# A fused cross-attention, mixer and mixture-of-experts block: weighing ahead of the scores in a head slot, and the split of keys and values moved

## The reference

```
Q = (layernorm(x) @ Wq.T + bq);  K = ctx @ Wk.T + bk;  V = ctx @ Wv.T + bv
weights = softmax(Q K^T / sqrt(32))          # per batch and head, 128 x 2048
x = x + (weights V) @ Wo.T + bo
```

## Time and profile before

| | |
|---|---|
| median of 3 executions | 2321.56 us (2314.86 to 2323.9) |
| the profiled execution, its own time | 2320.49 us |
| its span in the trace | 2318.7 us |
| attention slots of batches 0 to 6 | about 151 to 1091 us of the span |
| attention slots of the last batch | about 1091 to 1241 us |
| PE busy over the span | 1967.2 us (85%) |
| VectorE, GpSimd, ScalarE busy | 1543.6, 1149.4, 804.4 us |

### The profile page before, as it was taken

How to read it: one execution, slowest core, us unless ns; L and a number is a source line. 1 busy time by engine, 2 the same in 40 slices (tenths; PEclk the granted TensorE clock), 3 DMA queues, 4 the chain that set the end, 5 groups by cost and what they waited for, 6 DMA issues and landing times. The chain is left out here.

```text
span 2318.7 us, 39327 instructions
## 1 busy us (share of the span) xinstructions
PE 1967.2 (85%) x14449; PEld 1291.3 (56%) x14449; DVE 1543.6 (67%) x1595; ACT 804.4 (35%) x1127; POOL 1149.4 (50%) x809
## 2 busy tenths in 40 slices
PE   6989999999999999999555895666656666899999
PEld 3867777777777777776443673111111112468874
DVE  5136766666666766676553742999969996645654
ACT  1134444444444444443221334333353332023320
POOL 3136666666666666665444101666546663231200
PEclk9999999999999999999557996889969888989999
DMA  4554555555555555554114105000400003101100
GB/s 168 157 155 149 176 169 169 165 170 173 158 172 170 171 155 175 172 171 128 64 58 143 37 0 154 0 1 0 127 19 0 0 0 115 37 1 50 63 5 36
DMA packets 182665, 233.75 MB, mean 101 GB/s; under 512 B 20976, under 2 KB 111856, under 8 KB 176208
## 3 DMA queue, kind: packets, MB, share of 16 engines
q1 hardware_dynamic: 182480, 231.23, 31.9%
HBM read 157.62 MB, written 73.53 MB: 100 GB/s over the span
## 5 line engine op out<-in xcount | busy, mean ns | idle before, releaser
L368 POOL TENSOR_TENSOR a_half<-a_pt 128x1024 f32<-128x1024 f32 x128 | 307.1, 2400 | 374.5 <-ACT a_pt L418 374.5
L1031 PE MATMUL s_ps<-s_seen,s_ident 128*128 128x512 f32 x512 | 322.2, 733 | 186.5 <-DVE s_seen L981 186.2
L918 POOL TENSOR_TENSOR s_drive<-s_du,s_bc 128x512 f32<-128x512 f32 x256 | 324.2, 1270 | 260.9 <-DVE s_ps L973 143.4
L418 ACT ACTIVATE a_pt<-a_shift 128x2048 f32<-128x2048 f32 x128 | 245.1, 1915 | 556.8 <-PE a_o L600 461.5
L487 DVE TENSOR_TENSOR a_shift<-a_s,a_neg_rows 128x2048 f32<-128x2048 f32 x128 | 293.4, 2292 | 195.8 <-ACT a_neg_rows L430 195.8
L474 DVE TENSOR_REDUCE a_top<-a_s 128x128 f32<-128x2048 f32 x128 | 293.1, 2290 | 74.9 <-PE a_s L575 74.8
L1031 PEld LDWEIGHTS s_ps<-s_seen,s_ident 128*128 128x128 f32 x512 | 88.1, 215 | 422.1 <-DVE s_seen L981 384.7
L973 DVE TENSOR_TENSOR_SCAN s_ps<-s_ps,s_drive 128x512 f32<-128x512 f32 x256 | 310.8, 1214 | 2.9 <-ACT s_ps L947 2.9
L947 ACT ACTIVATE s_ps<-s_delta,s_a_neg 128x508 f32<-128x508 f32 x256 | 175.8, 688 | 295.5 <-DVE s_ps L973 295.2
L575 PE MATMUL a_s<-a_q_stack,a_stack 32*128 32x128 f32 x4096 | 163.9, 301 | 49.0 <-DVE a_shift L487 40.2
L534 PE MATMUL a_pj<-p_c_hi,p_wk_hi 128*128 128x512 f32 x448 | 198.0, 442 | 0.0
(11 more groups left out here) (189 smaller groups left out, 3144.1 us busy)
## 6 DMA issues: line engine op xcount, KB each, us to landing
kv_scratch<-a_k_new SPq DMA_DIRECT2D x128, 256.0 KB, 2.5
kv_scratch<-a_v_new SPq DMA_DIRECT2D x128, 256.0 KB, 3.6
a_stack<-kv_scratch SPq DMA_DIRECT2D x512, 64.0 KB, 2.2
a_v<-kv_scratch SPq DMA_DIRECT2D x32, 1024.0 KB, 5.9
a_raw<-in_ctx SPq DMA_DIRECT2D x120, 256.0 KB, 3.3
s_bc<-bc_scratch SPq DMA_DIRECT2D x32, 512.0 KB, 6.1
a_q_stack<-q_scratch SPq DMA_DIRECT2D x128, 64.0 KB, 2.1
e_ew_raw<-in_ew SPq DMA_DIRECT2D x8, 1024.0 KB, 4.8
```

The lines of the kernel that those rows point to most:

```text
L368: nc.gpsimd.tensor_tensor(half[:], w[:, 0:2], w[:, 2:4], ALU.add).then_inc(halved, 1)
L418: nc.scalar.activation(pt_head(g, p), shift[:].rearrange("p (i n) -> p i n", n=BANK), ACT.Exp).then_inc(exped, 1)
L918: nc.gpsimd.tensor_tensor(drive[:, s % RS], du[:, s // N], bc[:, 0, n, :], ALU.mult).then_inc(driven, 1)
L1031: pe.matmul(ps[:, i, :], ident[:], seen[:, s % 2], start=(n == 0), stop=(n == N - 1))\
```

## The change

It rewrites only PE's slot. `weigh` now stands ahead of the wait for `shifted` and of the scores. All twelve key matmuls stand ahead of `turn_top` (before: six), the first six value matmuls stand between `turn_top` and `turn_negative` (before: the last six of the keys), and the last six value matmuls stand behind `turn_negative` (before: all twelve). The wait for `v_out`, by which the PSUM tile of the values is free again, moves with the first of them. Nothing is added or removed.

```diff
-            def keys(b, c, p, out, ks):
+            def keys(b, c, p, out):
...
-            def values(b, c, p, out):
+            def values(b, c, p, out, ks=range(KC)):
...
                 more = projects or h + 1 < H
+                if g >= 1:
+                    weigh(b, g - 1, p, first)
+                elif not first:
+                    weigh(b - 1, GROUPS - 1, p, False)
                 if more:
                     pe.wait_ge(shifted, n)
                     if h + 1 < H:
                         scores(b, h + 1)
                     else:
                         scores(b + 1, 0)
-                if g >= 1:
-                    weigh(b, g - 1, p, first)
-                elif not first:
-                    weigh(b - 1, GROUPS - 1, p, False)
                 if projects:
                     if p == 0:
                         split_done(b + 1, g)
                     pe.wait_ge(k_out, H * (b + 1) + HG * g + p)
-                    keys(b + 1, g, p, p_ps[:, 0], range(2))
+                    keys(b + 1, g, p, p_ps[:, 0])
                 if more:
                     turn_top(n)
                 if projects:
-                    keys(b + 1, g, p, p_ps[:, 0], range(2, KC))
+                    pe.wait_ge(v_out, H * (b + 1) + HG * g + p)
+                    values(b + 1, g, p, p_ps[:, 1], range(2))
                 if more:
                     turn_negative(n)
                 if projects:
-                    pe.wait_ge(v_out, H * (b + 1) + HG * g + p)
-                    values(b + 1, g, p, p_ps[:, 1])
+                    values(b + 1, g, p, p_ps[:, 1], range(2, KC))
```

More of the change, by code:

```diff
@@ L540, in split_done @@
                 pe.wait_ge(clo_out, KC * (CH * b + c - AHEAD + 1))
-            def keys(b, c, p, out, ks):
+            def keys(b, c, p, out):
+                part_of = slice(p * P, (p + 1) * P)
+                for k in range(KC):
+                    mm = three(out, wk_hi[:, k, part_of], wk_lo[:, k, part_of], c_hi[:, c % 2, k, :], c_lo[:, c % 2, k, :],
+                               k == 0, k == KC - 1)
+                mm.then_inc(projected, 1)
+            def values(b, c, p, out, ks=range(KC)):
                 part_of = slice(p * P, (p + 1) * P)
                 for k in ks:
-                    mm = three(out, wk_hi[:, k, part_of], wk_lo[:, k, part_of], c_hi[:, c % 2, k, :], c_lo[:, c % 2, k, :],
+                    mm = three(out, c_hi[:, c % 2, k, part_of], c_lo[:, c % 2, k, part_of], wv_hi[:, k, :], wv_lo[:, k, :],
                                k == 0, k == KC - 1)
@@ L563, in _ @@
                         pe.wait_ge(k_out, t // 2 - 1)
-                    keys(0, c, p, s_ps[:, t % CH, :], range(KC))
+                    keys(0, c, p, s_ps[:, t % CH, :])
                     if t >= CH:
```

## The result

| | before | changed |
|---|---|---|
| median | 2322.73 us (4 runs) | 2435.26 us (4 runs, 2431.62 to 2441.0) |
| ratio | 1 | 1.0498, 95% interval 1.0482 to 1.0515 |
| profiled execution, its span | 2318.7 us | 2433.5 us |
| granted clock, mean of the span | 0.926 | 0.907 |

What follows compares the result with a forecast made beforehand. The softmax's ring between engines was taken to set the slot, with PE almost without room beside it. Terms of 77, 39 and 6 us sum to 122 on 2320.5 us, giving 2442; range 2398 to 2484.

Steps and rivals of the forecast that it cites:

- Twelve keys ahead of the first turn: PE's projecting slots: first turn 3.99 us behind the scores instead of 3.63, making the slot 8.44 us against 8.10.
- The exponentials gain nothing in projecting slots: ScalarE's exponentials start earlier, worth up to 0.3 us at the widening, but nothing was booked in projecting slots.
- p = 3: Slot where the sums follow the weighing: with a matmul shape change of 0.1 to 0.2, 8.8 us against 8.69.
- The stall at p = 0: Weighing waits for out_ready and holds the scores: slot 10.9 us against 8.60.
- The loop: PE's own loop at batch turns falls into idle time before out_ready: 6 us back over six passes.
- first term: Longer slots over the groups, less the loop's 6 us back: +77 us.
- The clock: PE's 2.7 us gap once a group drops it to 1.2 GHz: 1.5 us for each of 26 gaps, +39 us.
- second term: The lower clock behind PE's 26 gaps: +39 us, with 0 to 80 possible.
- clock stays up: Rival: one gap in a group is not enough to drop PE's clock, 2403 us; chance 0.18.
- falls for longer: Rival: each clock drop outlasts the ring's first half, 3 us a gap, 2481 us and somewhat over; chance 0.14.
- The last batch: 11 slots gain 0.5 us each, four at p = 0 lose 12 us together: +6 us.

Runs made afterwards that it cites:

- finish_early: Changed kernel with VectorE's finish_group moved ahead of shift_scores in slots with p = 3; 2332.61 us, ratio 1.006 to the kernel before.
- refit_split: Changed kernel with finish_early's edit and nine, six and nine matmuls ahead of, between and behind the turns; 2339.75 us, ratio 1.0095 to the kernel before.
- clock_filled: Changed kernel with nine extra matmuls before the wait for out_ready at p = 0 of projecting slots; 2405.57 us, ratio 1.038 to the kernel before.
- split_only: Changed kernel with the weighing put back behind the scores, keeping only the new split of keys and values; 2464.28 us, ratio 1.0627 to the kernel before.

## Why the prediction was right, point by point

Predicted 2442 us, measured 2435: 122 us more than before against 115 between the spans of the two traces. The mechanism was right term by term; that the sum is so near is in part luck, since some errors cancel.

*Twelve keys ahead of the first turn.* Expected 3.99 us from scores to turn, measured 3.97; slot 8.44, measured 8.40. finish_early shows it without the stall: the slots stay at 8.41 instead of 8.11. That the late turn makes the 0.3 us is read from the trace (3.97 + 1.49 + 0.60 + 2.29 + 0.06 is 8.41); no run moves it by itself, since in refit_split the scores came late instead.

*The exponentials gain nothing in projecting slots.* Right: in the changed kernel they start 0.16 us behind the pass (536.19), and the second turn still comes 1.49 us behind the first. In the last batch, where nothing stands between the turns, the gain is there.

*p = 3.* Expected 8.8, measured 8.60. The 0.1 to 0.2 for the change of matmul shape came from no row. The changed kernel's trace has 0.33 us from the last value matmul to the weighing (513.62 to 513.95) where 0.23 is the pace, so 0.1 is there; but the weighing takes only 0.89 to the sums (513.95 to 514.84), not 1.01, and the two cancel.

*The stall at p = 0.* Expected 10.9 us without the clock; clock_filled shows 10.8, and finish_early takes the stall away.

*The loop.* Expected 6 us back. Before, the boundary slots inside the loop were 9.12, 9.64, 8.83, 9.12 and 9.26 us, on average 0.6 above 8.60, so only 3 us were there to win; the row that I had read, 9.64, was the longest. After, they are 12.05 to 12.3, no longer than the other slots with p = 0. That they were hidden is right. From the first pass of batch 0 to the first of the last batch, the two traces differ by 109 us, clock included; the prediction had 77 + 39 = 116. What the 25 slots with p = 0 at the lower clock have above 10.8 us is 37 us. That leaves 72 for the first term's 77: its slots were put too long, above all at p = 3, and the 3 us of loop that were not there to win offset part of that.

*The clock.* Expected 1.5 us for each of 26 gaps, 39 us; measured 1.4 us for nearly all of 25. Filling the gaps gave back less than their sum, since at the loop's boundaries the added matmuls stand behind the loop's own gap: those five slots are still 11.97 to 13.82 us long. The granted clock over the long stretch is 0.96 and not 0.93. The 0.93 did not follow from my own term: 1.5 us lost at half the clock are 3 us at 1.2 GHz in 37.6, which makes 0.96. The section that I cited (the Trainium skill, TensorE: Matmul & The Clock Gate, "HAM oscillation — how this bites in real kernels") has it right in kind. But the waits that it draws between its bursts are about 3 to 5 us long, and here 2.67 us were enough; so "by it the second term stands" claimed more than it says. The rivals "clock stays up" (2403) and "falls for longer" (2481) are both excluded by this.

*The last batch.* Expected +6, measured +4.7: from its first pass to its last 144.4 us (1200.83 to 1345.22) instead of 139.7 (1090.76 to 1230.48). Both parts hold: the four slots with p = 0 are 11.8 us longer in sum (12 expected), the eleven others 7.1 shorter (5 to 6 expected).

## What to carry to other kernels

Before moving an operation ahead on an in-order engine, list every semaphore that it waits for and where its producer stands: here, in one slot of four, the operation moved ahead waited for the same engine as the work that it overtook, but for a later instruction of it. Where a ring between engines sets the time, count for each of its steps whether the engine is free when the step is due; filler work has to be divided by these gaps, and of the divisions run here the best was the one there was (six, six, twelve, with the weighing behind the scores). And a stall may hide others, so the gain of removing it is smaller than the stall: here the loop's 1.8 us came to light. Last, an order that is wrong where the engine is full can be right where it has room: the weighing ahead of the scores pays in the last batch alone.

## What the runs showed of the hardware that I had not expected

The drop of the clock was regular. In the changed kernel nearly every slot with p = 0 from the first batch's last group on is 12.05 to 12.4 us long (one is 13.68: there the scores and five keys behind them are slow too), while the first one that had the gap, in batch 0, is 10.71 us, about as in clock_filled. So a gap of 2.5 to 2.7 us once in a group was followed by a lower clock in 25 of 26 cases, though PE is busy in between. The regular gaps of 1.3 us in every slot of split_only never were.

Between the two, at the loop's boundaries, the length of the last gap alone does not decide. In split_only the clock fell behind gaps of 1.77, 1.96 and 1.80 us (slots of 11.49, 11.68 and 11.48 us) and not behind 2.27 and 1.69 (10.40 and 9.83). In finish_early it fell behind 1.84 and 2.12 us and not behind 1.78, 2.17 and 1.80. What does decide was not tried, nor whether the regularity in the changed kernel comes from the length of the group.
